# Cross-attention and MX feed-forward layer on one core: x transposed by DMA in 128-row tiles, FFN weights returned in twelve pieces, FFN inputs loaded in the last quad

## The reference, cut to what matters

```python
x = x + xattn(layernorm(x), ctx)        # softmax(q k^T / sqrt(128)) v, then Wo
x = x + ffn(layernorm(x))

def ffn(x):                             # I = 2048
    gate = mx_linear(x, w_gate)         # both operands quantized in blocks of 32
    up = mx_linear(x, w_up)             # along the last axis, with a shared power of two
    return mx_linear(silu(gate) * up, w_down)
```

## Time and profile before

| | us |
|---|---|
| median of 3 runs | 2155.86 (2154.7 to 2156.72) |
| the profiled execution | 2156.28 |
| its span, first to last instruction | 2154.7 |

### The profile page before, as it was taken

How to read it: one execution, slowest core, us unless ns; L and a number is a source line. 1 busy time by engine, 2 the same in 40 slices (tenths; PEclk the granted TensorE clock), 3 DMA queues, 4 the chain that set the end, 5 groups by cost and what they waited for, 6 DMA issues and landing times. The chain is left out here.

```text
span 2154.7 us, 47837 instructions
## 1 busy us (share of the span) xinstructions
PE 2069.8 (96%) x15818; PEld 1530.8 (71%) x15818; DVE 1538.8 (71%) x3455; ACT 1024.8 (48%) x2760; POOL 795.3 (37%) x1093
## 2 busy tenths in 40 slices
PE   6899999999999999999999999999999978899996
PEld 5678788787878787878787878888788853344442
DVE  6777777777777777777777767776665547988884
ACT  7765555454555555545454545554444432222331
POOL 4323333333333333333333333331111005777774
PEclk9999999999999999999999999999999999999998
DMA  6743333333333333333333333332323253454554
GB/s 218 183 85 74 77 77 77 77 77 74 77 75 77 77 77 77 77 77 77 75 79 77 77 63 77 77 72 65 60 63 64 52 152 67 80 91 85 85 90 68
DMA packets 398590, 179.26 MB, mean 83 GB/s; under 512 B 361984, under 2 KB 374784, under 8 KB 398400
## 3 DMA queue, kind: packets, MB, share of 16 engines
q1 hardware_dynamic: 375616, 125.10, 29.2%
q0 software_dynamic: 16608, 45.36, 8.4%
q10 hardware_dynamic: 6176, 6.29, 1.0%
HBM read 61.08 MB, written 27.26 MB: 41 GB/s over the span
## 5 line engine op out<-in xcount | busy, mean ns | idle before, releaser
L562 ACT ACTIVATE qk<-b_qk 128x512 f16<-128x512 f32 x256 | 152.7, 596 | 607.9 <-PE b_s L1011 607.9
L860 DVE TENSOR_REDUCE nmax<-b_s 128x2 f32<-128x512 f32 x257 | 177.7, 691 | 334.7 <-PE b_s L1011 308.9
L1011 PE MATMUL b_v<-attn_weights,kvT 128*128 128x256 f16 x3072 | 377.2, 273 | 8.5 <-POOL attn_weights L392 8.5
L1011 PE MATMUL b_qk<-xT,attn_weights 128*128 128x256 f16 x3072 | 380.8, 274 | 1.8 <-DVE xT L708 1.7
L1011 PE MATMUL b_qk<-kvT,attn_weights 128*128 128x256 f16 x3072 | 378.3, 273 | 0.0
L884 DVE SCALAR_TENSOR_TENSOR psplit<-prob,rrec,psplit 128x256 f16<-128x256 f32 x514 | 287.2, 600 | 80.1 <-ACT psplit L603 80.1
L1011 PEld LDWEIGHTS b_v<-attn_weights,kvT 128*128 128x128 f16 x3072 | 300.3, 98 | 44.2 <-issue 9.5
L1011 PEld LDWEIGHTS b_qk<-xT,attn_weights 128*128 128x128 f16 x3072 | 302.2, 98 | 39.1 <-DVE xT L708 2.4
L1011 PEld LDWEIGHTS b_qk<-kvT,attn_weights 128*128 128x128 f16 x3072 | 301.3, 98 | 35.5
L603 ACT ACTIVATE psplit<-prob,rrec 128x256 f16<-128x256 f32 x514 | 233.0, 500 | 109.8 <-DVE rrec L877 109.3
L593 ACT ACTIVATE prob<-b_s,nmax 128x256 f32<-128x256 f32 x514 | 239.2, 470 | 56.1 <-DVE nmax L860 26.9
(11 more groups left out here) (124 smaller groups left out, 2747.3 us busy)
## 6 DMA issues: line engine op xcount, KB each, us to landing
ffn_w<-wffn SPq DMA_DIRECT2D x48, 256.0 KB, 3.1
acc<-xtok POOLq DMA_DIRECT2D x16, 512.0 KB, 4.2
out<-acc POOLq DMA_DIRECT2D x16, 512.0 KB, 3.8
out<-attn_weights POOLq DMA_DIRECT2D x32, 256.0 KB, 4.5
xrow<-xq POOLq DMA_DIRECT2D x61, 128.0 KB, 3.7
kvrow<-kvt POOLq DMA_DIRECT2D x61, 128.0 KB, 3.3
stage<-wattn SPq DMA_DIRECT2D x12, 512.0 KB, 4.0
ffn_scratch<-ffn_t SPq DMA_DIRECT2D x48, 128.0 KB, 1.8
```

The source lines that it names most:

```text
L562: eng.activation(dst, src, ACT.Copy, scale=scale).then_inc(sm[done], 1)
L860: eng.tensor_reduce(nmax[:, :], bS[:, :].rearrange("p (q f) -> p q f", q=2), AX_X, ALU.max, negate=True).then_inc(sm["max_done"], 1)
L1011: last = eng.matmul(out, l, r, start=(a == 0), stop=(a == len(pairs) - 1))
```

## The change

1. x goes through in 128 rows every second quad (thirty times, m = 0 to 29). Even quad: mean and variance at k = 0, POOL's rstd, normalization by DVE at k = 3, high part by ACT at k = 3, from the normalized rows before any transpose, into a new buffer xsplit. Odd quad: POOL loads the next 128 rows, DVE makes the low part at k = 0, and SP issues a DMA transpose of both parts into xT after the probabilities' transpose of k = 1. PE's transposes are gone; PE waits at each batch's first quad for two more such transposes.
2. The FFN weights return in twelve pieces of four tiles: eight in quad 62 (two after each k), four in quad 63 (one after each k). They lie in chunk 1 and half of chunk 2; the stage's buffers move to the other half and to free pieces of chunk 0.
3. The first two `load_x_tile` stand in quad 63, behind its transposes of k = 0 and k = 1.
4. `x_clip` of a batch's second tile moves from k = 3 to k = 1.
5. Loops of ACT and SP have two quads in their bodies; quads 0 to 3 are written out on ACT and DVE.

```diff
-LAST_STEPS = {5: (1, 2), 6: (1, 3), 8: (2, 2), 9: (2, 3), 11: (3, 2), 13: (3, 3), 15: (4, 3)}
+LAST_STEPS = {5: (1, 2), 6: (1, 3), 8: (2, 2), 9: (2, 3), 11: (3, 2), 13: (3, 3), 15: (4, 1)}
...
-        xrow = sb("xrow", D, F32, ROWS)
-        xnorm = sb("xnorm", D, F32, ROWS)
+        xrow = sb("xrow", D, F32)
+        xnorm = sb("xnorm", D, F32)
+        xsplit = sb("xsplit", 2 * D, F16)
...
+        inter = free_part(2, 1, 0, 4).bitcast(F32)
+        iqT = free_part(2, 1, 4, 4).bitcast(BF16)
+        sil = free_part(0, 0, 0, 2).bitcast(F32)
+        iq = free_part(0, 0, 3, 2).bitcast(BF16)
+        i8 = free_part(0, 0, 5, 1).bitcast(FP8)
+        dsum = free_part(0, 1, 0, 2).bitcast(F32)
+        xqT = free_part(0, 1, 3, 1).bitcast(BF16)
...
-        FW = 2 * 2 * WCHUNK
+        FW = 2 * WCHUNK
...
+            def transpose_x(m):
+
+                wait_apart(eng, "x_lo", m + 1)
+                eng.dma_start_transpose(xT[:, bass.ds(((m + 2) & 3) * 1024, 1024)].rearrange("p (j f) -> p j f", j=8),
+                                        xsplit[:, :]).then_inc(sm["xT_loaded"], 16)
+
...
+            def ffn_quad(n, store=True, load=True, m=None):
                 for k in range(QUAD):
                     transpose_p(4 * n + k, k % 2)
+                    if m is not None and k == 1:
+                        transpose_x(m)
                     if store and k == 0:
                         store_ffn(n - FFN_FROM - 1)
                     if load and k == 1:
...
+            for k in range(QUAD):
+                transpose_p(4 * (NQ - 1) + k, k % 2)
+                if k < 2:
+                    load_x_tile(k, k)
+            transpose_p(4 * NQ, 0)
+
...
-            load_x_tile(0, 0)
-            transpose_p(4 * NQ, 0)
-            load_x_tile(1, 1)
             tile(0, 0)
             tile(1, 1)
...
-            def prep(r):
-                rstd(ROWS, 1, "aggr_done", "rstd_step", "rstd_done", r)
-                wait_apart(eng, "xn_ready", r + 1)
-                load_x(r + 1)
+            def prep(r, m, odd):
+                if odd:
+                    wait_apart(eng, "xn_ready", m + 1)
+                    load_x(m + 1)
+                else:
+                    rstd(P, 1, "aggr_done", "rstd_step", "rstd_done", m)
...
             def x_prep(m):
-                hi(prep_slot(xT, m + QPB, 0), bX[:, 0:KC * ROWS].rearrange("p (c f) -> p c f", c=KC), X_SCALE,
-                   "x_tr", m + 1, "x_hi")
+                if not isinstance(m, int) or m > 0:
+                    eng.wait_ge(sm["xT_loaded"], 16 * m)
+                hi(x_part(0), xnorm[:, :].rearrange("p (c f) -> p c f", c=KC), X_SCALE, "xn_ready", m + 1, "x_hi")
...
+            def load_resident(w0, quads, done):
+
+                eng.wait_ge(sm["v_done"], 4 * quads)
+                eng.wait_ge(sm["o_done"], 4 * quads)
+                eng.dma_start(fw[:, w0 * 512:(w0 + 4) * 512].rearrange("p (w f) -> p w f", w=4),
+                              wqs[w0:w0 + 4].rearrange("w p f -> p w f")).then_inc(sm[done], 16)
+
...
-                    if prepare and k == 2:
-                        x_prep(n)
+                    if m is not None and k == 3:
+                        x_prep(m)
+                    if resident:
+                        w0, each, done = resident
+                        for a in range(each):
+                            load_resident(w0 + 4 * (each * k + a), n, done)
...
-            load_resident(0, 32, NQ - 1, "gate_up_resident")
-            quad(NQ - 1, prepare=False)
-            load_resident(32, FFN_TILES, NQ, "down_resident")
+            quad(NQ - 3, prepare=False)
+            quad(NQ - 2, prepare=False, resident=(0, 2, "gate_up_resident"))
+            quad(NQ - 1, prepare=False, resident=(32, 1, "down_resident"))
...
-                if q == 4 and k == 3:
+                if q == 4 and k == 1:
                     x_clip(2 * b + 1)
...
-                    if prepare and k == 0:
-                        x_stats(n)
+                    if prepare and k == 0 and odd:
+                        x_lo(m)
+                    if prepare and k == 0 and not odd:
+                        x_stats(m)
...
-                    if prepare and k == 3:
-                        x_lo(n)
+                    if prepare and k == 3 and not odd:
+                        x_apply(m)
...
-                    if prepare and k == 1:
-                        x_apply(n)
...
-                    if prepare and k == 2:
-                        x_transpose(n)
...
-            def ready(n):
-                eng.wait_ge(sm["x_lo"], n)
+            def ready(n, first):
+                if first:
+                    eng.wait_ge(sm["xT_loaded"], 8 * n)
                 eng.wait_ge(sm["kv_lo"], n)
```

More of the change, by code:

```diff
@@ L295, in ffn_quad, with odd @@
                         load_ffn(w + 1)
+            def odd(n):
+                return (n - 1) // 2 if n % 2 and n < NQ - 4 else None
             for n in range(QPB):
@@ L304, in _ @@
             ffn_quad(FFN_FROM, store=False)
[L305 to L309, removed]
-                ffn_quad(n, store=False, load=False)
-            for n in range(NQ - 4, NQ):
-                ffn_quad(n, store=False, load=False)
+            ffn_quad(FFN_FROM + 1, m=odd(FFN_FROM + 1))
+            with eng.Fori(FFN_FROM // 2 + 1, FFN_TO // 2 - 1) as m:
+                ffn_quad(2 * m)
+                ffn_quad(2 * m + 1, m=m)
+            for n in range(FFN_TO - 2, FFN_TO + 2):
+                ffn_quad(n, store=(n <= FFN_TO), load=(n < FFN_TO - 1), m=odd(n))
+            with eng.Fori(FFN_TO // 2 + 1, NQ // 2 - 2) as m:
+                ffn_quad(2 * m, store=False, load=False)
+                ffn_quad(2 * m + 1, store=False, load=False, m=m)
             def load_x_tile(t, at):
@@ L322, in load_x_tile @@
                                         ).then_inc(sm[f"xqT_loaded{at}"], 16)
+            for n in range(NQ - 4, NQ - 1):
+                ffn_quad(n, store=False, load=False)
+            for k in range(QUAD):
[3 more added lines that the diff above has]
+            transpose_p(4 * NQ, 0)
             def transpose_inner(v, at):
@@ L582, in kv_prep, with quad @@
                    "kv_loaded", 16 * (m + 1), "kv_hi")
[L584 removed]
+            def load_resident(w0, quads, done):
[3 more added lines that the diff above has]
+                              wqs[w0:w0 + 4].rearrange("w p f -> p w f")).then_inc(sm[done], 16)
+            def quad(n, front=True, split=0, ffn=False, prepare=True, m=None, resident=None):
                 for k in range(QUAD):
@@ L650, in _, with even @@
                 split_piece(0, pc)
[L651 to L663 removed]
+            def even(n):
+                return None if n % 2 else n // 2
+            for n in range(QPB):
+                quad(n, split=QUAD // 2 if n == QPB - 1 else QUAD, m=even(n))
+            quad(FFN_FROM, m=even(FFN_FROM))
+            quad(FFN_FROM + 1, ffn=True)
+            with eng.Fori(FFN_FROM // 2 + 1, FFN_TO // 2) as m:
+                quad(2 * m, ffn=True, m=m)
+                quad(2 * m + 1, ffn=True)
+            quad(FFN_TO, ffn=True, m=even(FFN_TO))
+            quad(FFN_TO + 1)
+            with eng.Fori(FFN_TO // 2 + 1, NQ // 2 - 2) as m:
+                quad(2 * m, m=m)
+                quad(2 * m + 1)
+            quad(NQ - 4, prepare=False)
             eng.wait_ge(sm["ffn_stored"], 16 * FFN_TILES)
[L665 to L667 removed]
+            quad(NQ - 3, prepare=False)
+            quad(NQ - 2, prepare=False, resident=(0, 2, "gate_up_resident"))
+            quad(NQ - 1, prepare=False, resident=(32, 1, "down_resident"))
             quad(NQ, front=False, prepare=False)
@@ L854, in quad @@
                 w = n - FFN_FROM
+                m, odd = 2 * s + q // 2, q % 2
                 ends = q == QPB
@@ L937, in _ @@
                 split_piece(0, pc)
-            quad(0, split=QUAD)
-            with eng.Fori(1, QPB - 1) as n:
-                quad(n, split=QUAD)
-            quad(QPB - 1, split=QUAD // 2)
+            for n in range(QPB):
+                quad(n, split=QUAD // 2 if n == QPB - 1 else QUAD, s=0, q=n)
             quad(FFN_FROM, ffn=True, s=0, q=QPB)
@@ L1012, in product @@
                 return last
-            def x_transpose(m):
-                eng.wait_ge(sm["xn_ready"], m + 1)
-                wait_apart(eng, "x_lo", m)
-                for c in range(KC):
-                    last = eng.transpose(bX[:, c * ROWS:(c + 1) * ROWS], xnorm[:, c * P:(c + 1) * P],
-                                         ident[0:ROWS, 0:ROWS])
-                last.then_inc(sm["x_tr"], 1)
             def ffn_rhs(tile0, c):
```

82 lines of the change are left out of this document (26 added, 56 removed).

## The result

| | before | after |
|---|---|---|
| median, us | 2155.28 (2154.55 to 2156.72, 4 runs) | 2092.52 (2090.5 to 2094.3, 4 runs) |
| the profiled execution | 2156.28 | 2090.5 |
| its span | 2154.7 | 2088.9 |

The ratio is 0.9708, interval 0.9691 to 0.9725: 62.8 us less. The forecast was 2101 (55 less), its range 2088 to 2116.

The account below looks back on a forecast made before the run. The prediction took PE's summed instructions to bound the attention stage, with slack only at the ends. Terms 30.0 + 9.0 + 7.2 - 1.2 + 8.6 + 1.4 = 55.0 us off the profiled 2156.28 gave 2101, range 2088 to 2116 (from bounds: 2090 to 2112).

Parts of the forecast that it names:

- part 1: Attention stage: x transposed by DMA takes 60 groups of four transposes off PE; 30.0 us less, bounds 26 to 31.
- part 2: First quads: PE's four waits for weight pieces split by POOL go; 9.0 us less, bounds 2 to 14.
- the stops stay: zero: DVE's loop end: its stops with nothing to wait for remain; zero change, bounds -4 and +6.
- part 3: Quads 62 and 63: twelve weight pieces remove the 4 MB load's stall; 7.2 us less, pieces cost 1.2.
- part 4: FFN inputs transposed in quad 63: PE's wait and half clock go; 8.6 us less, bounds 6.3 and 9.5.
- part 5: FFN stage's start: earlier clip and rescale end a DVE wait; 1.4 us less, bounds 0 and 2.
- (a): First quads don't improve, another stop replacing each; part 2 gives 2 us or less, total 2109; chance 0.14.
- (b): Quad 62: pieces delay transposes as the 4 MB did; 28.8 us instead of 1.2, total 2129; chance 0.04.
- (c): ACT's longer two-quad loop stops for instructions at its 26 turns; costs 23 us, total 2124; chance 0.06.
- (d): Late x transpose queues probabilities of k = 2 behind it; 120 us more, total 2221, slower; chance 0.03.
- (e): Transposes off, PE waits as long for something else at k = 2; only 25 us gained, 2131; chance 0.05.

Follow-up runs that it names:

- experiment 1: Kernel before, with 80 idle semaphore increments put ahead of all DVE work: 2147.41 us, ratio 0.9962 to before.
- experiment 4: Kernel before, with POOL's wait for normalized rows and next x load moved behind the k = 0 weight piece in quads 0 to 3: 2145.17 us, ratio 0.9948.
- experiment 7: Changed kernel, with 17 semaphore increments spread over DVE's loop body, making it 308 instructions instead of 291: 2095.07 us.
- experiment 3: Changed kernel, with FFN weights loaded whole, first FFN inputs late and the clip back at k = 3: 2108.86 us, ratio 0.9786 to before.
- experiment 5: Changed kernel, with one clip alone moved back from k = 1 to k = 3: 2097.98 us.
- experiment 11: Kernel before, with the clip alone moved from k = 3 to k = 1: 2151.42 us, ratio 0.9983 to before.
- experiment 8: Changed kernel, with FFN weights loaded whole (4 MB behind quad 62, 2 MB behind quad 63), early inputs and clip kept: 2100.58 us.
- experiment 2: Changed kernel, with 60 semaphore increments put in front of DVE's work at the start: 2096.36 us, ratio 0.9723 to before.
- experiment 9: Changed kernel, with the first two FFN input loads back behind the last probability transposes: 2096.25 us.
- experiment 6: Changed kernel, with the FFN weight pieces issued by SP behind each probability transpose instead of by ACT: 2089.84 us, ratio 0.9695 to before.
- experiment 10: Kernel of experiment 6, with ACT preparing POOL's weight piece before DVE's in quads 0 to 3: 2115.42 us.

## Why the prediction was right, and where it was wrong

The sign and the main term were right, and the forecast was 8.5 us too high at the median. By its own steps, on the profiled executions:

| term | forecast | measured |
|---|---|---|
| part 1, transposes off PE (60 of close to 0.50) | 30.0 | 29.8 |
| part 2, POOL in the first quads | 9.0 | 4.8 |
| "the stops stay: zero" | 0 | 15.2 |
| part 3, 4 MB stall less the pieces' own cost | 7.2 - 1.2 = 6.0 | 3.5 |
| part 4, FFN inputs | 8.6 | 9.1 |
| part 5, the clip | 1.4 | 3.4 |
| sum | 55.0 | 65.8 |

- **Part 1** held. The 29.8 are the heads of before added up (27.8 for 56 groups) and 2.0 taken for the four groups in the first quads. The kernels of experiment 1 and after, both without stops that reach PE, agree: 1549.01 - 1521.46 = 27.6. DVE, ACT and SP took the new work without cost: x's transposes land after a median of 3.1, and the heads of the loop are 6.53 us, or 6.76 with an FFN transpose, and almost none waits.
- **Part 2.** The term is right for the cause it names: removed by itself (experiment 4) it gave 10.1. In the changed kernel four waits of b_qk for POOL's pieces, 3.0 us, took the old ones' place, and the first stage is 2.8 us longer than in experiment 4 although it has no transposes. Those heads, 6.8 to 7.6 us, are not explained to the end: changing ACT's order made them worse. The rule from the Trainium skill that the prediction weighed here (SBUF — State Buffer, "SBUF: two separate sides") would have left the term at 2 us: the runs with 10.1 and 4.8 decide against that result, though not against the shared port.
- **"The stops of DVE at its loop's end stay."** This is the step that failed, by 15.2 us against bounds of -4 and +6. The prediction read the nine stops as a fixed cost and charged PE 0.82 for one of them; it did not add up the heads at the turns (13.9 us in before) and did not see the second kind of stop at the statistics. The stops hang on two things that the change moved by the way. One is where the loop's code lies: 80 idle instructions ahead of it took all of them off (experiment 1), while a start 9.6 us earlier with the code in its place took none (experiment 4). 17 more instructions inside the loop of the changed kernel brought none back (experiment 7). The other is what stands last ahead of the turn: with the clip there, nine stops are seen, without it none or one, in both kernels (experiments 3, 5 and 11); this holds for the stops ahead of nmax, not for those at the statistics. Part 1 alone had taken off the stops at the statistics (experiment 3: 14.4 of the 15.2 us). Whether by the new place of the loop or by the statistics' new shape and order in it stays open. That the stops are fetches of instructions at a taken branch, as the Trainium skill describes them (Runtime: NRT & Kernel Launch, "Instruction fetch mechanics"), fits experiments 1 and 7, but no run shows the fetch itself.
- **Part 3.** The 7.2 of the stall came back when the loads were made whole (a head of 15.17 in experiment 8). The 1.2 for the pieces was mis-sized: 0.3 per head was taken from a landing of 5.4, and the transposes landed in 4.8 to 6.9, median 6.1, the upper bound of the prediction's own estimate. It cost 3.9, just inside its bound of 4, and this was luck of the execution: in experiments 2, 5, 7 and 9, with the same order of issue, quads 62 and 63 took 58.4 to 62.3 us, 6.2 to 10.0 above the 52.28 of undisturbed heads, and transposes landed after up to 8.6.
- **Part 4.** The number came out and its reason did not. The pieces alone took the stage to the last context product from 21.81 to 15.02 (experiment 9), the early inputs alone to 17.48, since the 2 MB load then stalls the last probabilities (experiment 8); both together to 12.75. At the median the early inputs are worth 3.7 beside the pieces. Two terms were summed that share one cause.
- **Part 5.** 1.3 at DVE's first clips of the FFN stage, as forecast. The hidden stops were in no step. The other 2.1 us of the row have no cause that a run shows; the lower clock behind the later wait is not it (experiment 5).
- **Rivals.** (a) is half true, see part 2; it doesn't decide, since the stops outweigh it. (b) didn't come, though other executions came nearer to it than this one: transposes landed after 6.9 at most here, 8.6 in experiment 5. (c), (d) and (e) didn't come: ACT's loop stops nowhere, x's transposes land after 4.8 at most, and the cadence is 6.53. The count in (c), 190 instructions in DVE's loop, takes only those that the profile lists as busy; the body has 308.
- **The range.** The bounds of the terms, plainly added, give 2086 to 2122 and not 2090 to 2112; the prediction doesn't say how it narrowed them. The result lies in either.

Undone one at a time, the pieces are worth 8.1, the clip 5.5 and the inputs 3.7, together 17.3; experiment 3, without all three, stands 16.3 above the changed kernel.

## What to carry to other kernels

Where the trace shows stops "for issue" at the turns of a long loop, add up the steps of the bound engine around the turns, and try a shift of the code and another last instruction before believing the stop to be fixed: here 15 us hung on it. A bulk load beside a latency-bound transfer should be issued right behind that transfer and in pieces that land before the next one; when it is issued matters as much as how large it is. Before summing two terms, ask whether both count the same load being out of the way.

## What the runs showed of the hardware

- Stops of 2.5 to 4.5 us on DVE at the turn of a loop of 291 or 308 instructions and, in that of 308, 1.8 to 2.2 us a little later in the body. In the kernel before both vanish when 80 instructions stand ahead (experiment 1) and stay when the start alone is 9.6 us earlier (experiment 4).
- The same wait of PE, 3.14 us at the same place of the program, was followed by 5 us at a granted clock of 1.00 in after and in experiments 6 and 9, and of 0.66 in experiment 10 and 0.71 in experiment 8. In experiment 8 nothing of it was left 18 us later, since PE then waited less for DVE.
- A transpose that lands in 3.1 us with 1 MB issued right behind it takes a median of 6.1 when 1 MB is issued from ACT in the same moment, and up to 8.6 in other executions of the same order.
- Eighty increments of an idle semaphore ahead of DVE's first work lengthened the time to i = 16 by 6.7 us, sixty by 4.7. DVE's first instruction began at 10.08 and at 7.79 us: 0.11 us for each of the 20 between them.
